# A decoder kernel on one core: the first group's first norm in one pass, its scale and shift behind the transposes

## The reference

```
def layer_norm(x, g, b, eps=1e-05):
    m = jnp.mean(x, -1, keepdims=True)
    v = jnp.mean(jnp.square(x - m), -1, keepdims=True)
    return (x - m) * jax.lax.rsqrt(v + eps) * g + b

for i in range(DEPTH):
    x = x + self_attention(layer_norm(x, ln1_g[i], ln1_b[i]), Wq[i], Wk[i], Wv[i], Wo[i], bo[i])
    h = layer_norm(x, ln2_g[i], ln2_b[i])
    x = x + (gelu(h @ W1[i] + b1[i]) @ W2[i] + b2[i])
```

## Time and profile before

| | us |
|---|---|
| median of 3 runs | 958.55 |
| lowest, highest | 957.61, 958.65 |
| the profiled execution, own time | 958.88 |
| its span, first to last instruction | 957.0 |

### The profile page before, as it was taken

The page is one execution under the profiler, slowest core; times in us unless marked ns, Lnnn a source line. Parts: engine busy times, 40 slices in busy tenths (PEclk is TensorE's granted clock), DMA queues, the critical chain, the costliest instruction groups (busy, mean ns, idle before and its releaser), DMA issues.

```text
span 957.0 us, 21341 instructions
## 1 busy us (share of the span) xinstructions
PE 944.3 (99%) x8394; PEld 815.4 (85%) x8394; DVE 672.8 (70%) x1531; ACT 612.4 (64%) x1387; POOL 480.0 (50%) x381
## 2 busy tenths in 40 slices
PE   7999999999999999999999999999999999999998
PEld 4687888888888889888888888888997889998997
DVE  7696868677677868696777668776662676766445
ACT  3777777786867867777778676786856345444220
POOL 3437365456836472776466366816247224006453
PEclk9999999999999999999999999999999999999999
DMA  6221000001110000021000002000028597720001
GB/s 211 88 91 45 2 17 2 4 15 51 40 45 18 2 1 18 1 89 45 8 11 2 18 2 82 6 2 7 2 57 203 135 203 147 177 50 1 23 23 45
DMA packets 71582, 47.56 MB, mean 50 GB/s; under 512 B 44511, under 2 KB 68159, under 8 KB 71487
## 3 DMA queue, kind: packets, MB, share of 16 engines
q1 hardware_dynamic: 71487, 46.27, 18.6%
HBM read 44.16 MB, written 2.10 MB: 48 GB/s over the span
## 4 chain that ended last, share of the span: by engine, by line
PE 94%; DVE 4%; ACT 1%; issue 1%; DMA 1%; POOL 0%; SPq 0%; POOLq 0%; DVEq 0%; ACTq 0%
PE F L1464 21%; PE F L1618 19%; PE A L1464 16%; PE A L1805 5%; PE A L1798 5%; PE A L1563 4%; PE A L1958 4%; PE A L1521 3%; PE A L1580 2%; PE A L1478 2%; PE F L1478 2%; PE F L1457 2%; PE A L1554 1%; PE A L1457 1%; PE A L1537 1%; PE A L1674 1%
## 5 line engine op out<-in xcount | busy, mean ns | idle before, releaser
L1464 PE MATMUL F<-xt,w 128*128 128x512 f32 x864 | 217.8, 400 | 0.2 <-ACT scratch L1221 0.2
L475 POOL TENSOR_TENSOR ht<-scratch,ht 128x512 fp32r<-128x512 f32 x128 | 176.0, 1396 | 29.4 <-ACT ht L1224 27.9
L1464 PEld LDWEIGHTS F<-xt,w 128*128 128x128 f32 x864 | 157.6, 188 | 38.2 <-issue 3.0
L1618 PE MATMUL F<-w,ht 128*128 128x256 f32 x1536 | 188.8, 282 | 0.0
L1618 PEld LDWEIGHTS F<-w,ht 128*128 128x128 f32 x1536 | 182.8, 188 | 5.3 <-issue 4.6
L463 POOL TENSOR_TENSOR rstd<-var,minus_half 128x4 f32<-128x4 f32 x32 | 37.6, 1174 | 178.8 <-DVE var L611 178.1
L1221 ACT ACTIVATE scratch<-F,b_now 128x512 f32<-128x512 f32 x128 | 87.7, 685 | 36.6 <-POOL ht L475 19.1
L1464 PE MATMUL A<-wa,xt 128*128 128x512 f32 x372 | 89.8, 397 | 0.0
L470 POOL TENSOR_TENSOR x<-x,vec_f 128x1024 f32<-128x1024 f32 x16 | 38.0, 2376 | 94.0 <-DVE scratch L631 94.0
L1224 ACT ACTIVATE ht<-scratch 128x512 fp32r<-128x512 f32 x128 | 81.1, 634 | 4.0
L1464 PEld LDWEIGHTS A<-wa,xt 128*128 128x128 f32 x372 | 69.0, 188 | 15.9 <-issue 0.2
(11 more groups left out here) (264 smaller groups left out, 2040.3 us busy)
## 6 DMA issues: line engine op xcount, KB each, us to landing
raw_f<-in_L_attn_W_dram SPq DMA_DIRECT2D x8, 1024.0 KB, 5.5
scratch<-in_L_ffn_fc_B_dram SPq DMA_DIRECT2D x32, 256.0 KB, 4.4
scratch<-in_L_ffn_fc_A_dram SPq DMA_DIRECT2D x32, 256.0 KB, 3.9
raw_f<-in_L_ffn_fc_A_dram SPq DMA_DIRECT2D x32, 64.0 KB, 3.2
scratch<-in_x_dram SPq DMA_DIRECT2D x1, 2048.0 KB, 11.0
raw_f<-in_L_ffn_fc_B_dram SPq DMA_DIRECT2D x32, 64.0 KB, 3.2
x<-in_x_dram SPq DMA_DIRECT2D x3, 512.0 KB, 3.7
out_dram<-x SPq DMA_DIRECT2D x3, 512.0 KB, 2.9
```

The source lines that it names most:

```text
L475: pool.tensor_tensor(ht[:, 1, m, :], hf[:, m % 2, :], ht[:, 0, m, :].bitcast(F32), ALU.subtract).then_inc(h_lo, 1)
L1464: last = pe.matmul(out, lhs(a, c), rhs(b, c), start=clear and k == 0, stop=k == len(total) - 1, skip_group_check=not clear)
L1618: last = pe.matmul(F[:, t % 2, 0:D], ht[:, a, c, P * t:P * t + P], w2[:, b, c, :], start=k == 0, stop=k == len(passes) - 1)
```

## The change

The first group of the first layer is normed in one pass, (x - mean) * rstd, with two values per partition, into `xh[0]`, without g and b. As the channels lie on the partitions behind the transposes, g and b become one value per partition there, and are applied as the PSUM banks are read: by ScalarE in the same instruction that makes the high part, and by VectorE into a full-precision copy (`full`, in the memory of `xh[1]`), from which the low part is then taken. The two engines take the banks in opposite order, and semaphores keep them out of the same bank at a time. g and b are loaded once more for this, one value per partition (`col_a`, 256 single values each), behind the weights of q and k; the repeated rows in `vec_a`, which all other groups still use, are loaded behind the token columns. The fillers are 1 and 4 where they were 5 and 3. Five load semaphores become three that count two loads each.

```
-            load_vec(sp, 0, 0)
             load_a(sp, 0, 0)
+            for i, src in enumerate((ln1_g, ln1_b)):
+                sp.dma_start(col_a[:, i, :], src[bass.ds(0, 1)].rearrange("a (c p) -> p (a c)", p=P),
+                             allow_slow_non_contiguous=True).then_inc(col_loaded, 16)
             load_a(sp, 0, 1)
+            load_vec(sp, 0, 0)
...
             ln_moments(dve, 0, 0, 0, True)
-            ln_centred(dve, 0, 0, 0, 0)
-            ln_shifted(dve, 0, 0)
+            dve.wait_ge(ln_rstd[0], 1)
+            for t in range(TILES):
+                last = dve.tensor_scalar(xh[0][:, t, :], x[:, t, :], mv[0][:, t, 0:1], rstd[0][:, t:t + 1],
+                                         ALU.subtract, ALU.mult)
+                last.then_inc(ln_ready[0], 1)
+            dve.sem_inc(ln_xhat[0], 1)
...
             lo(dve, wa[:, 1, :, 0:2 * P], raw_a[:, :, 0:2 * P], wa[:, 0, :, 0:2 * P]).then_inc(wa_qk_ready, 1)
-            dve_xt_lo(dve, 0, 0)
+            dve.wait_ge(col_loaded, 32)
+            full = [xh[1].rearrange("p t d -> p (t d)")[:, TOK * c:TOK * c + TOK] for c in range(DC)]
+            dve.wait_ge(xt_psum[0], 2)
+            for c in (1, 0):
+                if c == 0:
+                    dve.wait_ge(xt_hi[0], 1)
+                dve.tensor_scalar(full[c], xt_bank(0, c, 0), col_a[:, 0, c:c + 1], col_a[:, 1, c:c + 1],
+                                  ALU.mult, ALU.add).then_inc(xt_full, 1)
+            for c in range(DC):
+                dve.wait_ge(xt_full, 2 - c)
+                dve.wait_ge(xt_hi[0], c + 1)
+                lo(dve, xt[0][:, 1, c, :], full[c], xt[0][:, 0, c, :]).then_inc(xt_lo[0], 1)
...
-            act_xt_hi(act, 0, 0)
+            act.wait_ge(col_loaded, 32)
+            for c in range(DC):
+                if c == 1:
+                    act.wait_ge(xt_full, 1)
+                act.wait_ge(xt_psum[0], c + 1)
+                act.activation(xt[0][:, 0, c, :], xt_bank(0, c, 0), ACT.Identity, bias=col_a[:, 1, c:c + 1],
+                               scale=col_a[:, 0, c:c + 1]).then_inc(xt_hi[0], 1)
...
             pe.wait_ge(ln_rstd[0], 1)
-            pe_busy(pe, F[:, 1, :], 5)
+            pe_busy(pe, F[:, 1, :], 1)
...
                 first_xt()
-                pe_busy(pe, F[:, 1, :], 3)
+                pe_busy(pe, F[:, 1, :], 4)
```

The merged semaphores, of which this is one of three places:

```
-            pool.wait_ge(bout_loaded, 16)
+            pool.wait_ge(wout_bout_loaded, 32)
```

More of the change, by code:

```diff
@@ L60, in build @@
         vec_a = sb("vec_a", [P, 3, D])
+        col_a = sb("col_a", [P, 2, DC])
         vec_f = sb("vec_f", [P, 3, D])
@@ L191, in build @@
                              "top_wcol", "index_ready"))
-        x0_loaded, wv_loaded, wout_loaded, ctx_loaded, bout_loaded = (
-            sem(n) for n in ("x0_loaded", "wv_loaded", "wout_loaded", "ctx_loaded", "bout_loaded"))
+        x0_loaded, wv_ctx_loaded, wout_bout_loaded = (sem(n) for n in ("x0_loaded", "wv_ctx_loaded", "wout_bout_loaded"))
+        col_loaded, xt_full = sem("col_loaded"), sem("xt_full")
         big_loaded = [sem(f"big_loaded{r}") for r in range(4)]
@@ L291, in _ @@
                     (x_loaded[0], x_loaded0_late)[b], 16)
+            load_a(sp, 0, 0)
+            for i, src in enumerate((ln1_g, ln1_b)):
+                sp.dma_start(col_a[:, i, :], src[bass.ds(0, 1)].rearrange("a (c p) -> p (a c)", p=P),
+                             allow_slow_non_contiguous=True).then_inc(col_loaded, 16)
+            load_a(sp, 0, 1)
             load_vec(sp, 0, 0)
-            load_a(sp, 0, 0)
-            load_a(sp, 0, 1)
             for f, lg in enumerate((fc1_logits, fc2_logits)):
@@ L305, in _ @@
             load_bias(sp, 0, 0)
-            sp.dma_start(wv_raw, Wkv.rearrange("(c p) n -> p c n", p=P)[:, :, 1024:2048]).then_inc(wv_loaded, 16)
+            sp.dma_start(wv_raw, Wkv.rearrange("(c p) n -> p c n", p=P)[:, :, 1024:2048]).then_inc(wv_ctx_loaded, 16)
             load_w1(sp, 0, first=True)
@@ L311, in _ @@
             sp.wait_ge(wo_ready, 1)
-            sp.dma_start(wout_raw, Wout.rearrange("(j p) n -> p j n", p=P)).then_inc(wout_loaded, 16)
+            sp.dma_start(wout_raw, Wout.rearrange("(j p) n -> p j n", p=P)).then_inc(wout_bout_loaded, 16)
             load_w2(sp, 0)
@@ L329, in _ @@
             sp.wait_ge(wo_ready, DEPTH)
-            sp.dma_start(ctx_raw, ctx_in.rearrange("b t d -> t b d")).then_inc(ctx_loaded, 16)
+            sp.dma_start(ctx_raw, ctx_in.rearrange("b t d -> t b d")).then_inc(wv_ctx_loaded, 16)
             sp.wait_ge(biased[0], 4 * DEPTH)
             sp.wait_ge(ln_ready[0], TILES * ITEMS * DEPTH)
-            sp.dma_start(vec_a[:, 0, :], bout.rearrange("(a n) -> a n", a=1).broadcast_to([P, D])).then_inc(bout_loaded, 16)
+            sp.dma_start(vec_a[:, 0, :], bout.rearrange("(a n) -> a n", a=1).broadcast_to([P, D])).then_inc(wout_bout_loaded, 16)
             sp.wait_ge(w2_ready, DEPTH)
@@ L1695, in first_step @@
                 pe_busy(pe, A[:, 1, :], 1)
-                pe.wait_ge(wv_loaded, 16)
+                pe.wait_ge(wv_ctx_loaded, 16)
                 wvt_turn(0)
@@ L1726, in first_step @@
                 pe.wait_ge(wvt_out, 4)
-                pe.wait_ge(wout_loaded, 16)
+                pe.wait_ge(wout_bout_loaded, 16)
                 value_output(*range(0, 4))
@@ L1761, in context @@
             def context():
-                pe.wait_ge(ctx_loaded, 16)
+                pe.wait_ge(wv_ctx_loaded, 32)
                 for c in range(DC):
```

## The result

The changed kernel takes 961.26 us, median of 9 runs (960.52 to 962.90); the kernel before, run beside it, 958.61 (957.61 to 959.26). The ratio is 1.0028, 95% interval 1.0019 to 1.0037: slower by 2.65 us, where 1.05 less was forecast. The profiled execution took 961.31, with a span of 959.4.

A forecast was written before the change was run, and what follows sets the result against it. TensorE bounds the kernel, so an earlier first product moves the end as much: 1.27 less 0.3 gives 1.0 us off 958.88, 957.9; the runs' median lies 0.33 below, so 957.5, with 956.5 to 959.6 for 8 in 10.

The forecast's parts named there:

- step 7: GpSimd's set-up beside the four new norm instructions: port collisions cost 0.3 us, bounds 0 and 0.98.
- step 10: Load semaphores: renamed and merged, they wait for the same loads in the same places, costing nothing.
- step 3: Transposes: the last ends 0.40 us behind the last norm, at 8.84, with one filler matmul in front instead of five.
- steps 1 and 5: Norm starts at 7.05, not 7.30; VectorE's PSUM scale-and-shift takes 0.68 per chunk, first product 2.99 behind last norm.
- 2: VectorE's norm: eight instructions become four, 1.39 us undisturbed, ending at 8.44 instead of 10.81, 2.37 sooner.
- the rival of the low level: TensorE still at 1.2 GHz at the first products: twelve cost 2.2 us more, net 1.2 slower, 959.8; 10%.
- 4: Low part of Wq and Wk, 0.68 us, follows the norm directly; its high part is ready at 7.9, so hidden.
- the rival at 15%: One real hit of 0.98 on GpSimd's port at the norm instead of 0.3 leaves 0.3 gained: 958.2; 15%.
- 6, 8, 9: Later weights hidden; SP's loads 1.2 us later at no cost; column loads land 6.4 to 8.3, hidden by 0.5.
- The clock rival's sign: At the start of TensorE's products: the clock is wrong if the first six take over 1.7 us.
- the gain is absorbed by a late load: A later wait that no row shows as tight, b1 or x, absorbs the gain: 958.5; 8%.
- the 1.27: TensorE's first product at 11.43 against 12.70, 1.27 us sooner, before the 0.3 for collisions is taken off.

The follow-up runs named there:

- e1: Kernel before plus an unused tensor of 16 bytes per partition where the change puts its column vectors, later tensors 32 bytes higher: 960.80 us, ratio 1.0024.
- e2: Changed kernel with `col_a` allocated last, so all other tensors lie as before: 958.81 us, ratio 1.0002.
- e3: e2 with GpSimd's top-k set-up held back until the four one-pass norm instructions are done: 957.75 us, ratio 0.9986.
- e6: Kernel before with at alone, the last tensor, moved by 32 bytes: 960.26 us, ratio 1.0015.
- e5: Kernel before with ht moved by 32 bytes against multiples of 128 and everything behind it 128 bytes higher: 961.50 us, ratio 1.0028.
- e9: e3 with xt and the small tensors in front of it 96 bytes lower, `b1_rows` moved behind at: 953.05 us, ratio 0.9942.
- e7: e3 with ht moved from 96 to 64 against multiples of 128, everything later 128 bytes higher: 959.41 us, ratio 1.0006.

## Why the prediction was wrong

The forecast was 1.05 us down; it came out 2.65 up. In the profiled executions 957.9 was predicted and 961.31 taken, 3.4 apart: 1.1 at the first product (11.73 with the 0.3 of step 7, against 12.83), 2.2 that grow behind it, and 0.1 at the end. The failed step, for the sign, is **step 10**, and the frame around it: it listed the renamed semaphores as all that was left, and no step costed the declaration of `col_a`, 2.2 of the 3.4. Of the 1.1 at the first product, step 7 is 0.63 and step 3 is 0.57; steps 1 and 5 give back 0.10. I read the diff for what is executed and not for what is allocated. "Everything behind 12.70 hangs on semaphores, so an earlier first product moves the end by as much" was right as far as it goes, but takes the pace behind as given. e1 and e2 show the 2.2: 1.90 slower by the declaration alone, 2.45 faster without its effect. What step 10 did name costs nothing that can be measured: e2 has all the renamed semaphores and is at 1.0002 of the kernel before. (Of the three that are left of the five, two count two loads each, and not all three.)

The steps one by one:

1. Right: the norm starts at 7.03 (7.05).
2. 1.39 us undisturbed is right (e3: 1.38).
3. The transposes end 10.32, 0.97 behind the norm, where 0.40 was taken. In e2 it is 0.50 (six transposes 8.77 + 1.09 = 9.86, the norm 7.03 + 2.33 = 9.36). The difference of 0.47 is TensorE's pace: the four fillers next to them take 1.87 in the changed kernel, and 1.03 in e2 and e3. The granted clock reads 1.00 in all three, so only the pace shows it; 0.47 and 0.26 for one of 128x512 go with the low and the high level (1.2 and 2.4 GHz), as 0.45 and 0.245 do in the kernel before. So the rival of the low level did come true in part, ahead of the products where I had looked for it in them. e2 has the same code here and not this loss, so it differs from execution to execution.
4. Right: hidden. Wk's high part began at 6.10; the low part ran 9.28 to 9.96 behind the norm, ahead of the banks.
5. From last transpose to first product 2.51 us, 2.59 predicted, by misses that cancel, which is luck. VectorE began 0.10 behind the transposes, where I had 0.34, and its two PSUM instructions ended 0.13 later than taken; the sign for this step, other than 0.65 to 0.72, did show. The parts: the PSUM form takes 0.61 and 0.81 in the chain where I took 0.68 and 0.68 and 0.04 between (now 0.11), and ScalarE's two-operand form 0.78 where the plain copy was 0.61.
7. The mis-sized one: 0.93 us (2.32 - 1.39) for the collision where I took 0.3. That is nearly the upper bound of 0.98, the rival at 15%. The argument against it, that GpSimd's operations are short, failed: the first instruction stood still through a row of them. The argument from the old first pass compared two-tensor forms, which do not show this. In the old start it was GpSimd that was slower: its last two set-up rows (L510 and L514 there) took 0.42 and 0.96 beside these forms, and 0.23 and 0.53 in the changed kernel and in e3. I had not looked at that side.
6, 8, 9. Right: nothing waited for later weights, SP's queue or `col_a`; ScalarE was released by TensorE after 3.46, not by a load. So the descriptor per element, of which the Trainium skill warns (DMA: Bandwidth & Descriptors, "Rules for kernel authors"), cost nothing that this kernel shows. b1 was transposed at 23.62 and the next product for it came at 26.20, 0.10 later than before, the lag it had already.

```profile
23.62 0.24 PE L1716 MATMUL A<-ident,b_rows 32*128 32x32 f32 x1
...
26.20 1.64 PE L1503 MATMUL F<-xt,wa 128*128 128x512 f32 x6 [0.94 <-DVE xt L639]
```

The clock rival's sign, six first products in over 1.7, did not show (1.64). That the gain is absorbed by a late load did not happen either: what e3 gains at the first product over e2, 0.77, is 0.8 in the span.

One thing tempers the gain itself: the old start varies. Four profiled executions have it, and ln_b landed in 3.8 us (e6), 4.5 (e1), 4.9 (before) and 5.4 (e5), with the first product at 11.95, 12.30, 12.70 and 13.48. In e5 the granted clock was also at half from 9.82 to 13.23. The new start does not hang on that landing: e3's 11 runs lie within 0.5 us. So the 1.27 was counted from one draw out of a spread of 1.5. That e2 is no faster than before in the median, though its first product is at 12.38, fits such a spread; how much of the 1.27 was luck of that trace was not measured.

## What to carry over

A new tensor, however small, goes behind the ones that TensorE reads, or its effect on their places is part of the change: compare the busy time of unchanged matmul groups in both profiles first, since a gap that grows evenly through untouched code is pace and not a wait. When VectorE's work moves to one-source forms, look at what GpSimd does in those microseconds, and hold it back if it has time. A wait that differs from execution to execution is worth less than its length in the one trace at hand.

## What the runs showed that I had not expected

- The place of an operand in SBUF changes TensorE's pace: 372 products of wa and xt take 89.8, 89.2 or 87.4 us with xt at 224, 0 or 128 past a multiple of 256; 1536 of w2 and ht 188.3 to 191.9; 360 of wo and at 43.5 to 45.5. Between the best and the worst placement tried, with the same start, the kernel takes 953.05 and 959.41 (e9, e7), 0.7% apart.
- Where both operands begin at the same place within 256 bytes, products of 512 columns were at their fastest (390 ns against 395 to 397 for wa,xt) and products of 256 columns at their slowest (285 against 281 to 283 for w,ht), in all nine placements. What else decides stays open: xt's move slowed wo,at by 1.4 us, with neither operand moved.
- 256 single values per load cost SP 0.47 us of issue, less than the 0.59 of a 512 KB load of x, and landed in 2.8 and 3.0 us, by 6.4; the first reader came at 10.19.
- Five short GpSimd operations that overlap at their ends held one VectorE instruction up for 0.77 us.
